# VectorE packs the adjacency for the symmetry test in place of GpSimd, in a gated graph network kernel

## What is computed

```python
for _ in range(5):
    s_in = state @ in_W.T + in_b
    s_out = state @ out_W.T + out_b
    a_in = Af @ s_in
    a_out = AfT @ s_out
    a = concat([a_in, a_out, state])
    r = sigmoid(a @ r_W.T + r_b)
    z = sigmoid(a @ z_W.T + z_b)
    joined = concat([a_in, a_out, r * state])
    h_hat = tanh(joined @ h_W.T + h_b)
    state = (1 - z) * state + z * h_hat
out = tanh(state @ o1_W.T + o1_b) @ o2_W.T + o2_b
x = layernorm(x + out)
```

## Time and profile before

| | |
|---|---|
| median of 3 runs | 731.83 us |
| lowest and highest | 728.74 and 732.44 us |
| span of the profiled execution | 729.6 us (the profile gives no other time for it) |
| TensorE matmuls busy | 694.2 us, 95%, 3168 instructions |
| VectorE busy | 483.7 us, 66% |
| ScalarE busy | 238.9 us, 33% |
| GpSimd busy | 123.8 us, 17% |
| mean granted TensorE clock | 0.982 of full speed |

### The profile page before, as it was taken

The page is one execution under the profiler, slowest core; times in us unless marked ns, Lnnn a source line. Parts: engine busy times, 40 slices in busy tenths (PEclk is TensorE's granted clock), DMA queues, the critical chain, the costliest instruction groups (busy, mean ns, idle before and its releaser), DMA issues.

```text
span 729.6 us, 8541 instructions
## 1 busy us (share of the span) xinstructions
PE 694.2 (95%) x3168; PEld 575.3 (79%) x3168; DVE 483.7 (66%) x747; ACT 238.9 (33%) x369; POOL 123.8 (17%) x94
## 2 busy tenths in 40 slices
PE   7999999787999999999999999999999999998991
PEld 7878888566888888888888888888888888886881
DVE  4777767898866458754555865455586556657884
ACT  1755544422112215311222431222143112213553
POOL 0022013999940000000000000000000000005052
PEclk9999999979899999999999999999999999999997
DMA  8763632000000000000000000000000000030003
GB/s 283 259 225 107 201 104 69 1 0 1 0 1 1 0 1 1 0 0 0 0 0 0 0 0 0 0 0 0 0 0 1 0 1 1 0 115 1 1 1 117
DMA packets 18412, 27.25 MB, mean 37 GB/s; under 512 B 1872, under 2 KB 9424, under 8 KB 18384
## 3 DMA queue, kind: packets, MB, share of 16 engines
q1 hardware_dynamic: 16864, 26.48, 11.0%
q10 hardware_dynamic: 1520, 0.40, 0.3%
HBM read 24.78 MB, written 2.10 MB: 37 GB/s over the span
## 4 chain that ended last, share of the span: by engine, by line
PE 83%; DVE 10%; ACT 2%; DMA 2%; issue 1%; ACTq 0%; DVEq 0%; SPq 0%
PE bank L452 36%; PE bank L395 14%; PE bank L397 14%; PE bank L396 14%; PE bank L424 2%; PE bank L535 1%; DVE a L825 1%; DVE rows L806 1%; DMA a<-in_L_gnn_r_W_dram 1%; PE bank L547 1%; DVE work L867 1%; DVE work L873 1%; DMA stage<-in_adj_dram 1%; DVE ring L811 1%; DVE stateT L892 1%
## 5 line engine op out<-in xcount | busy, mean ns | idle before, releaser
L452 PE MATMUL bank<-ring,rows 128*128 128x512 f32 x1280 | 297.1, 392 | 1.1 <-ACT ring L620 0.9
L452 PEld LDWEIGHTS bank<-ring,rows 128*128 128x128 f32 x1280 | 240.6, 189 | 51.7 <-ACT ring L620 1.6
L654 ACT ACTIVATE work<-work,bias 128x512 f32<-128x512 f32 x120 | 86.6, 724 | 294.3 <-DVE work L867 293.6
L867 DVE SCALAR_TENSOR_TENSOR work<-degree,deg_w,bank 128x512 f32<-128x512 uint16 x120 | 88.8, 743 | 111.6 <-PE bank L397 111.1
L811 DVE CAST ring<-a 128x1024 fp32r<-128x1024 uint8 x128 | 97.8, 774 | 13.0 <-PE bank L452 13.0
L395 PE MATMUL bank<-u_c,fold 128*128 128x512 f32 x240 | 97.7, 407 | 3.3 <-DVE work L867 3.3
L397 PE MATMUL bank<-u_c,fold 128*128 128x512 f32 x240 | 94.6, 394 | 0.0
L396 PE MATMUL bank<-u_c,fold 128*128 128x512 f32 x240 | 94.6, 394 | 0.0
L357 POOL TENSOR_TENSOR a<-a,o_bb 128x1024 f32<-128x1024 f32 x4 | 10.9, 2760 | 448.4 <-DMA a<-in_x_dram 448.4
L395 PE MATMUL bank<-st_c,own 128*128 128x512 f32 x160 | 63.1, 394 | 3.1 <-DVE st_c L806 3.1
L397 PE MATMUL bank<-st_c,own 128*128 128x512 f32 x160 | 63.1, 394 | 0.0
(11 more groups left out here) (121 smaller groups left out, 803.0 us busy)
## 6 DMA issues: line engine op xcount, KB each, us to landing
stage<-in_adj_dram SPq DMA_DIRECT2D x28, 512.0 KB, 5.2
work<-in_x_dram SPq DMA_DIRECT2D x1, 2048.0 KB, 15.9
a<-in_x_dram SPq DMA_DIRECT2D x1, 2048.0 KB, 8.1
a<-in_adj_dram SPq DMA_DIRECT2D x3, 512.0 KB, 11.2
out_dram<-a SPq DMA_DIRECT2D x3, 512.0 KB, 3.0
a<-in_L_gnn_r_W_dram SPq DMA_DIRECT2D x1, 768.0 KB, 6.8
a<-in_L_gnn_z_W_dram SPq DMA_DIRECT2D x1, 768.0 KB, 8.9
stateT<-in_L_gnn_h_W_dram SPq DMA_DIRECT2D x1, 768.0 KB, 10.4
```

What stands on the lines that cost most here:

```text
L452: last = nc.tensor.matmul(u_bank[2 * (c % 2) + d][:, :], rows[:, part, j, d * P:(d + 1) * P], ring[:, p % RING, jj, :], start=(j == 0 and ...
L654: nc.scalar.activation(gates[:, g, e, :], gates[:, g, e, :], ACT.Tanh if g == H else ACT.Sigmoid, bias=bias[:, g, e:e + 1]).then_inc(gate_ ...
L867: nc.vector.scalar_tensor_tensor(out=gates[:, g, e, :], in0=degree[:, c * CW:(c + 1) * CW], scalar=deg_w[:, g, e:e + 1], in1=g_bank[s % 3] ...
```

## The change

GpSimd's 56 additions are removed. VectorE gets `pack(i)`, one instruction that shifts the accumulator left by one and ors the next block in, 28 in all. `pack(i)` stands in VectorE's `aggregate` behind the expansion and the split with the same count, four for each of chunks 1 to 3: twelve in step 1, twelve in step 2 and four in step 3. Since the count depends on the step, VectorE's loop over steps 1 to 3 is written out. TensorE's and ScalarE's programs stay as they are.

```diff
--- before.py
+++ after.py
@@ -138,6 +138,7 @@
 
         PACK = 8
         NPK = NB // PACK
+        N_PACKS = 2 * NPK * (PACK - 1)
         flat_stage = stage[:, :, :, :].rearrange("p s a w -> p (s a w)")
         pack_rows = flat_stage[:, 0:NPK * N // 4].bitcast(U32).rearrange("p (g w) -> p g w", g=NPK)
         pack_cols = flat_stage[:, NPK * N // 4:2 * NPK * N // 4].bitcast(U32).rearrange("p (b g w) -> p b g w", b=NB, g=NPK)
@@ -329,27 +330,6 @@
                     add(deg_sum[:, 0:w], src[:, 0:w], src[:, w:2 * w], deg_summed if level == len(TREE) - 1 else byte_sum)
                     n += level < len(TREE) - 1
 
-            pool.wait_ge(pair_ready, S_PAIR)
-            pool.wait_ge(pair_stored, S_PAIR)
-            n = 0
-            for g in range(NPK):
-                def row_block(k):
-                    return a8[:, :, PACK * g + k, :].bitcast(U32)
-
-                def col_block(k):
-                    m = PACK * g + k
-                    return a8[:, m // BC, :, m % BC * P:(m % BC + 1) * P].bitcast(U32)
-
-                for acc, block_of in ((pack_rows[:, g, :].rearrange("p (c w) -> p c w", c=NC), row_block),
-                                      (pack_cols[:, :, g, :], col_block)):
-                    for k in reversed(range(PACK - 1)):
-                        twice = block_of(PACK - 1) if k == PACK - 2 else acc
-                        wait(pool, packed, n)
-                        add(acc, twice, twice, packed)
-                        pool.wait_ge(packed, n + 1)
-                        add(acc, acc, block_of(k), packed)
-                        n += 2
-
             pool.wait_ge(o2_b_loaded, 16)
             pool.wait_ge(xr_loaded, 16)
             for c in range(NC):
@@ -824,6 +804,21 @@
                     dve.wait_ge(pair_stored, (IN_CHUNK_0 if q < NP else IN_CHUNK_1) + 1)
                 nc.vector.tensor_scalar(a8[:, c, 2 * p:2 * p + 2, :], staged[slot].bitcast(U32), 1.0, 0.0,
                                         ALU.mult, ALU.max, accum_out=above[:, q:q + 1]).then_inc(pair_stored, 1)
+
+            def pack(i):
+
+                kind, g = i // (PACK - 1) % 2, i // (2 * (PACK - 1))
+                k = PACK - 2 - i % (PACK - 1)
+                m = PACK * g + k
+                if kind == 0:
+                    acc = pack_rows[:, g, :].rearrange("p (c w) -> p c w", c=NC)
+                    first, block = (a8[:, :, b, :].bitcast(U32) for b in (PACK * g + PACK - 1, m))
+                else:
+                    acc = pack_cols[:, :, g, :]
+                    first, block = (a8[:, b // BC, :, b % BC * P:(b % BC + 1) * P].bitcast(U32) for b in (PACK * g + PACK - 1, m))
+                wait(dve, packed, i)
+                nc.vector.scalar_tensor_tensor(out=acc, in0=first if k == PACK - 2 else acc, scalar=1, in1=block,
+                                               op0=ALU.logical_shift_left, op1=ALU.bitwise_or).then_inc(packed, 1)
 
             def check_expand(n):
 
@@ -971,6 +966,11 @@
                         split_u(t, c - 1, n)
                     else:
                         split_state(t, c - 1, n - DB)
+                    i = ((t - 1) * (NC - 1) + c - 1) * 2 * DB + n
+                    if 0 <= i < N_PACKS:
+                        if i == 0:
+                            dve.wait_ge(pair_stored, S_PAIR)
+                        pack(i)
 
             def step(t, first=False, last=False):
                 if first:
@@ -990,7 +990,7 @@
                         expand(t, 1, p)
                 aggregate(t, 1, first)
                 if last:
-                    dve.wait_ge(packed, 2 * 2 * NPK * (PACK - 1))
+                    dve.wait_ge(packed, N_PACKS)
                     check_expand(0)
                     check_expand(1)
                 for c in range(NC):
@@ -1062,7 +1062,7 @@
             nc.vector.tensor_copy(ones_r[:, :], ones[:, :]).then_inc(ones_ready, 1)
             prepare()
             step(0, first=True)
-            with dve.Fori(1, LAST) as t:
+            for t in range(1, LAST):
                 step(t)
             step(LAST, last=True)
```

## The result

The changed kernel takes 712.38 us (median of 4 runs, 710.79 to 714.12), against 730.74 us for the kernel before measured beside it: a ratio of 0.9755, 95% interval 0.9723 to 0.9787. The forecast was 712.2 us in 708.5 to 716.5. A second measurement on another occasion gave 714.1 us and a ratio of 0.9758 (0.9733 to 0.9783).

A forecast was written before the change was run, and what follows sets the result against it. TensorE was taken to bound the kernel, held up in 126 to 209 us by VectorE instructions that GpSimd's SBUF reads stretch. From 731.83 us, -19.6 + 0 + 0 gave 712.2 us, range 708.5 to 716.5 us.

The forecast's parts named there:

- What bounds: Step 0's end and step 1's head, 126 to 209 us: GpSimd's SBUF reads stretch VectorE, TensorE loses 19.58 us.
- The sum: Whole run: -19.6 us for the additions, 0 for packs, 0 for the loop, giving 712.2 us.
- Step 0's own delay: Step 0's tail: degree row and degree copy delay the update, about 1.1 us of slack left, costed at nothing.
- The rival of a new wait: Step 0's tail, chunk 3's transpose: slack missing, TensorE waits some 1 us and loses clock, 716 us; chance 0.08.
- The packs: 28 VectorE packs in steps 1 to 3 at P = 0.60 us each, 16.8 us in all, hidden at no cost.
- The bound of 1.2 us: Chunks 2 and 3 of steps 1 and 2: pair 7's cast stays in time up to 1.2 us per pack.
- 2.9 us for each of four chunks: Chunks 2 and 3, steps 1 and 2: clock loss added once waits behind slow packs are long enough.
- the point at which packs would have eaten the gain: Slower rival, chunks 2 and 3 of steps 1 and 2: gain gone at P = 1.87 us per pack; chance 0.02.
- The written-out loop: VectorE's steps 1 to 3: register instructions go and the program grows, costed at 0 us.
- Busy shares: Rival, whole run: work moves from a 17% to a 66% busy engine, nothing returns, 731.8 to 733 us; chance 0.03.
- the rival of 1400 us: Packing not exact: flag set, general path computes everything again, over 1400 us; chance 0.01.
- after TensorE had been idle for 3 to 4 us: Step 0's tail: clock halves after such idling; 6 us at half rate give away 2.9 us each.

The follow-up runs named there:

- b_late: The kernel before with GpSimd's 56 additions held back by one whole step, to the same place in step 1: 731.3 us, ratio 0.9996.
- b_fill: The kernel before without packing, flag set to zero; GpSimd writes 130 back-to-back memsets instead, reading nothing: 712.39 us, ratio 0.9752.
- a_nopack: The changed kernel without its 28 packs and the wait for them, flag set to zero: 713.47 us, ratio 0.9778.
- a_two: The changed kernel with one more shift and or of the same size, into a spare tile, behind each pack: 712.56 us, ratio 0.9763.
- a_three: The changed kernel with two more shift and or instructions of the same size, into a spare tile, behind each pack: 723.3 us, ratio 0.99.
- b_unroll: The kernel before with only VectorE's loop over steps 1 to 3 written out, GpSimd still packing: 729.9 us, ratio 0.9991.
- after_again: The changed kernel itself measured once more, beside v_halves on one chip: 714.1 us, ratio 0.9758.
- b_paced: The kernel before with GpSimd's 56 additions spread over steps 1 to 3, each waiting for 1.5 more VectorE casts: 713.8 us, ratio 0.9768.
- v_halves: The changed kernel with the residual input loaded in two halves, so two of GpSimd's four residual additions run earlier: 708.48 us, then 709.6 us.
- v_halves_wait: v_halves with GpSimd's last two residual additions also waiting for the last chunk's fourth gate: 709.1 us, ratio 0.9703.

## Why the prediction was right, step by step

**What bounds.** It held: TensorE was held up by held VectorE instructions, in one stretch. b_late shows that they go with the additions, and b_fill that a GpSimd that is as busy but reads nothing costs no time.

**The sum.** -19.58 us was forecast from four transposes; on the same places the two profiles differ by 17.16 + 2.40 = 19.56 us. The span fell by 20.7 us; 1.4 us of that is the head, which began its first transpose at 122.57 instead of 123.95 us, and is no effect of the change. By the medians it is 730.74 - 712.38 = 18.4 us, and in the second measurement 730.51 - 714.1 = 16.4 us. That the forecast of 712.2 us lies within 0.2 us of the measured 712.38 us is partly luck: it started from 731.83 us, and measured beside the changed kernel the kernel before has 730.74 us.

**Step 0's own delay.** 1.1 us of slack were forecast in front of the transpose that stands in the gates of chunk 3, and no wait came: TensorE's list has none there. VectorE's last two additions of the update and that transpose, in the changed kernel:

```profile
143.99 1.28 DVE L887 TENSOR_TENSOR stateT<-stateT,work 128x512 f32<-128x512 f32 x2
```

```profile
146.49 0.60 PE L404 MATMUL bank<-ident,stateT 128*128 128x128 f32 x4
```

The additions end at 143.99 + 1.28 = 145.27 us, so 1.2 us of slack are left, as worked out. The rival of a new wait (716 us) did not occur.

**The packs.** P = 0.60 us was taken from the spacing of neighbouring instructions of the same length; the pack takes 684 ns, as the row taken for it (687 ns), and costs 0.0 us of the middle distance (a_nopack). The bound of 1.2 us is confirmed from both sides, by a_two (0.7 us in all) and a_three (9.4 us, where it gives 8.8). What I had added to it for the clock, 2.9 us for each of four chunks, did not come: waits of 0.7 and 1.0 us, with 2.1 us of matmuls between, left it at 1.00. So the point at which packs would have eaten the gain lay higher than I said, where the waits alone reach 19.6 us: at P = 1.2 + 19.6 / 12 = 2.8 us, unless longer waits bring the clock down after all, which was not tried.

**The written-out loop.** Costed at nothing, and b_unroll measures 0.9991.

**Busy shares.** The rival that went by them is out. VectorE has the same 66% in both profiles, and GpSimd at 17% was the cause. By the share of the whole run, which is what the Trainium skill, "Perfetto Trace Analysis", section "Identifying the Most-Contended Engine", goes by, GpSimd would not have been looked at. What found it was the stretch with gaps on TensorE, and to look for such gaps is what the next section of that page of the Trainium skill, "Optimization Strategy", asks for.

**The packing.** At 712 us the general path can't have run, so the flag stayed at zero, and the rival of 1400 us is out. That agrees with what the Trainium skill says in "DVE: scalar operands, raw-bit mode, write accounting and state across instructions", section "Raw-bit mode", but does not prove it: A is symmetric here, and a fault that changes the row pack and the column pack alike would leave the flag at zero too. No run has an A that is not symmetric.

**What I did not see.** That the move was not needed: spread out behind the casts, the same 56 additions on GpSimd give all but 0.35 us of the gain. And that the last step had the same fault, worth another 4 us of which the wait itself is 3.1, although I had read TensorE as busy throughout "from 209 us on"; its wait of 2.99 us stood in the profile of before too, outside the stretch that I had cut:

```profile
670.32 0.50 PE L395 MATMUL bank<-u_c,fold 128*128 128x512 f32 x1 [2.99 <-DVE work L867]
```

## What to carry to other kernels

An engine with a low share can be what holds up a kernel, if its work stands back to back beside a neighbour that it holds: look for a group whose mean duration changes between stretches, and for the instruction at which it changes back. Before moving such work, try to spread it and to keep it from beside the instructions that the busy engine waits for next: with both done, 56 additions cost 0.35 us in place of 19.6. Which of the two did it is open. And compare two profiles between fixed places in the middle: that told 0.4 us here, where two spans of the same kernel differ by 3.0 us.

## What the runs showed that I had not expected

- Waits of TensorE of 0.7 and 1.0 us, eight in a_three, left its clock at 2.4 GHz. A wait of about 3 us can go either way. In the first profile of the changed kernel the wait of 3.05 us in the last step ends at 649.45 us, and the stretch behind it still shows 1.00. In the second, of the same kernel, the same wait (3.08 us) ends at 651.22 us, and the clock is low behind it:

```profile
650.00:656.00 6.00, 6.00 (x28) 4.95 (x27) 3.98 (x7) 3.93 (x8) 0.00 (x0) 1.00 0.00 0
```

```profile
651.22:655.22 4.00, 4.00 (x11) 3.13 (x12) 2.50 (x4) 2.50 (x5) 0.00 (x0) 0.57 0.00 0
```

  Ten profiles here have this wait (2.88 to 3.08 us). The clock fell with it in five (after_again, a_nopack 2.94 us, b_paced 2.99 us, b_late, a_three) and stayed in the other five (before 2.99 us, after 3.05 us, b_unroll, b_fill, a_two). So its length does not decide. In the kernel before, the waits of 3.16 and 4.21 us were each followed by 1.2 GHz. What decides was not tried; my forecast's "after TensorE had been idle for 3 to 4 us" is too simple.
- GpSimd's memsets, back to back, hold only the casts (689 to 954 ns), and this costs nothing of the middle distance.
- The distance between fixed transposes repeats to 0.01 us over runs of different kernels (422.92 us in both profiles of the changed kernel, in b_fill, a_nopack, both of v_halves and v_halves_wait), while the first transpose comes anywhere from 122.57 to 126.26 us.
